# Splitting the rows of two gather layers into three bf16 parts, summed by three bf16 matmuls a column

## The chip, the core and the metric

The program runs on one core of one Trainium2 chip. Its engines are TensorE (PE; the profile lists its weight loads apart, as PEld), VectorE (DVE), ScalarE (ACT), GpSimd (POOL) and SyncE (SP), each with an instruction stream of its own; they meet only at semaphores. The metric is the device time of one execution, in microseconds (us); less is better.

## What is computed

A graph of 6250 nodes and 100000 edges, sorted by their end `dst`; a node has 256 features. After a layernorm and a relu come three SAGE layers, then a block of attention over the same edges. The three layers are what the change touches:

```python
def _sage_layer(x, src, dst, inv_deg, W_self, W_neigh, b):
    agg = jax.ops.segment_sum(x[src], dst, num_segments=N_NODES)
    mean = agg * inv_deg[:, None]
    return x @ W_self + mean @ W_neigh + b
deg = jax.ops.segment_sum(jnp.ones_like(src, dtype=features.dtype), dst, num_segments=N_NODES)
inv_deg = 1.0 / jnp.maximum(deg, 1.0)
h = relu(_sage_layer(features, src, dst, inv_deg, W0_self, W0_neigh, b0))
h = relu(_sage_layer(h, src, dst, inv_deg, W1_self, W1_neigh, b1))
h = _sage_layer(h, src, dst, inv_deg, W2_self, W2_neigh, b2)
```

## The kernel before

**Tiles, blocks and columns.** The nodes are NT = 49 tiles of 128. The edges are NB = 196 blocks of 512, and a block is BJ = 4 columns of 128 edges, one edge to a partition. Layer `l` (0, 1, 2; the title's two are 1 and 2) reads the rows `x[src]` out of a table in HBM, `tables[l]`, with one indirect DMA a column, issued by POOL (L763): 784 of them a layer. They land in `ring`, which has SLOTS = 7 slots of one block each.

**The sum over edges.** For a tile `t`, `sums(t)` on PE (L890 to L897) runs over the blocks that have edges of the tile. A block that lies over two tiles is walked twice, so a layer has 196 + 48 = 244 walks of 4 columns. For each column DVE makes a one-hot matrix (L842: edge by node of the tile), and PE multiplies it with the column's rows into `agg` (L895). One column of the rows' 257 words is the number 1, so the last column of `agg` is the node's degree. There are four one-hot buffers; DVE refills one when PE has used it (`onehot_used`).

**The rest of a tile.** DVE takes the mean (`means`, L948 to L953), PE transposes own rows and mean (`turn`, L904, L907), ACT copies them out (`take_turned`, L1016), PE multiplies with the weights (`products`, L913, L916), and ACT applies the relu into `h_nodes` (L1032). In the last layer the order is staggered over several tiles, and the projections of the attention (L1117 to L1168) run between.

**Who lets POOL go on.** SP relays: `landed` of a slot to PE (`rows_ready`, L790), and `onehot_used` to POOL (`slots_free`, L781), in one order: before it passes on block n it waits until block n + 4 - 7 has been used (AHEAD = 4).

**From one layer to the next.** The rows of a layer are the last layer's outputs, which ACT stores: eight tiles at a time, twice over, to `early_tables` (semaphore `stored`) and to `tables` (`last_stored`). The last tiles are stored one by one: tile 47 right behind its relu, tile 48 only to `tables`. The first LATE = 4 blocks of the next layer are gathered from `early_tables`, where tile 48's rows are zero, so POOL waits only for the stores of tiles 0 to 47; tile 48's rows are added into the ring afterwards, by one-hot matmuls on PE (`late_rows_tensor`, L717) and additions on DVE (`late_rows_vector`, L728). From the fifth block on POOL reads `tables` and waits for `last_stored`. The attention's gathers (L1278) start likewise from `vs_early`, stored by ACT at L1148. These are the lines of ACT's order at the end of layers 0 and 1, and POOL's first wait of a layer:

```python
                step(NT - 2)
                store(NT - 2)
                step(NT - 1)
                store(NT - 1)
...
                pool.wait_ge(W["stored"], since("stored", l, 0))
```

## Time and profile before

| | before |
|---|---|
| median of 3 runs (lowest to highest) | 4305.91 us (4305.18 to 4308.22) |
| the profiled execution, its own time | 4308.08 us |
| its span, first to last instruction | 4306.3 us |
| PE, DVE, ACT, POOL busy | 76%, 50%, 11%, 70% |
| mean granted TensorE clock | 0.89 of full |

The profiled execution's time is 1.8 us over its span, and 2.2 us over the median. POOL's busy time counts only the making of a DMA's descriptors; the 0.30 us between two gathers, in which it runs waits and register instructions, counts as idle "issue". In this execution layer 0's gathers end at 1018 us, layer 1's at 2000 us, layer 2's at 2982 us, and the attention's at 4018 us; what is behind is dense work. The page's chain covers only the last 20 us, so the place of the limit has to be read from the stages.

### The profile page before, as it was taken

Reading aid. Unit: us, or ns where it says so; the run is one execution under the profiler, and the core shown is the slowest. Engines: PE = TensorE matmul, PEld = TensorE weight load, DVE = VectorE, ACT = ScalarE, POOL = GpSimd, SP = SyncE. Lnnn points to the kernel's source line nnn. Section 1 sums busy time; section 2 is a strip of 40 time slices with the busy share of each in tenths; the row PEclk is TensorE's granted clock in tenths of the full one; section 3 lists DMA queues with packets and bytes.
Section 4 is the critical chain, followed back from the end, with each engine's and each line's share of the span. In section 5 each row is a group of like instructions: output and inputs, shape, how many; then the busy total and the mean of one; then the engine's idle time right before and its main releaser. Section 6 shows DMA issues by size and latency. Waiting matters only on the chain. (4 is left out here: it accounts for less than half of the span.)

```text
span 4306.3 us, 75198 instructions
## 1 busy us (share of the span) xinstructions
PE 3277.9 (76%) x13728; PEld 2372.7 (55%) x13729; DVE 2147.4 (50%) x6078; ACT 487.8 (11%) x1111; POOL 3020.7 (70%) x3154
## 2 busy tenths in 40 slices
PE   3777777777777777777788778887777777776798
PEld 2565555555555555555566555565655555555544
DVE  6434333333333333333455555545577777777733
ACT  4000000000000000000011101101011111111122
POOL 5777777777777777777777777776777777777200
PEclk9888889898888888888999999999888889898999
DMA  6444434435344344344444444445655555554411
GB/s 202 121 136 124 124 106 124 125 105 143 105 125 125 105 125 124 106 125 127 130 140 136 142 136 136 142 135 155 162 147 157 148 159 147 157 146 138 127 60 60
DMA packets 284796, 563.69 MB, mean 131 GB/s; under 512 B 104638, under 2 KB 176133, under 8 KB 279691
## 3 DMA queue, kind: packets, MB, share of 16 engines
q0 software_dynamic: 150528, 414.45, 34.0%
q10 hardware_dynamic: 70180, 89.46, 6.3%
q1 hardware_dynamic: 63974, 58.59, 4.4%
q8 instruction: 33, 0.54, 0.1%
q14 instruction: 81, 0.66, 0.0%
HBM read 487.19 MB, written 73.45 MB: 130 GB/s over the span
## 5 line engine op out<-in xcount | busy, mean ns | idle before, releaser
L763 POOL DMA_INDIRECT arena<-h_table,idx_v x2292 | 2174.3, 949 | 726.3 <-issue 694.0
L895 PE MATMUL banks<-arena 128*128 x5856 | 1544.9, 420 | 617.9 <-SPq L790 506.0
L895 PEld LDWEIGHTS banks<-arena 128*128 128x128 f32 x5856 | 1171.5, 208 | 957.2 <-issue 774.4
L842 DVE TENSOR_SCALAR arena<-iota_t,dst_e 128x128 f32<-128x128 f32 x2928 | 846.8, 310 | 821.7 <-PE banks L895 575.9
L1278 POOL DMA_INDIRECT arena<-vs_table,idx_v x764 | 765.0, 1001 | 232.8 <-issue 228.8
L1496 PE MATMUL banks<-arena 128*128 x1952 | 518.8, 416 | 52.8 <-DVE arena L1840 52.6
L1496 PEld LDWEIGHTS banks<-arena 128*128 128x128 f32 x1952 | 366.5, 199 | 192.5 <-issue 120.4
L916 PE MATMUL banks<-arena,lhs 128*128 128x256 f32 x1176 | 339.6, 439 | 5.0 <-ACT lhs L1016 0.2
L948 DVE TENSOR_SCALAR small<-banks 128x1 f32<-128x1 f32 x147 | 23.2, 158 | 638.7 <-PE banks L897 638.7
L1016 ACT ACTIVATE lhs<-banks 128x512 f32<-128x512 f32 x147 | 87.8, 597 | 2073.7 <-PE banks L907 2073.5
L916 PEld LDWEIGHTS banks<-arena,lhs 128*128 128x128 f32 x1176 | 240.5, 215 | 100.8 <-ACT lhs L1016 64.8
L1840 DVE SCALAR_TENSOR_TENSOR arena<-iota_n,tile_base,dst_e 128x256 f32<-128x256 f32 x488 | 224.0, 482 | 117.7 <-PE banks L1496 117.5
L1835 DVE TENSOR_TENSOR arena<-arena,banks (+1 forms) x196 | 238.9, 1219 | 31.0 <-issue 24.4
L907 PE MATMUL banks<-ident,tiles 128*128 128x128 f32 x294 | 69.4, 322 | 69.2 <-DVE tiles L953 69.2
L830 DVE TENSOR_SCALAR iota_t<-iota_n,tile_base 128x128 f32<-128x128 f32 x147 | 42.9, 292 | 153.5 <-issue 153.5
L913 PE MATMUL banks<-arena,ones_row 1*128 1x256 f32 x294 | 116.6, 480 | 0.0
L1125 PE MATMUL banks<-arena 128*128 128x512 f32 x196 | 92.3, 593 | 2.2 <-DVE arena L1158 2.2
L907 PEld LDWEIGHTS banks<-ident,tiles 128*128 128x128 f32 x294 | 36.0, 157 | 98.2 <-DVE tiles L953 98.2
L1968 PE MATMUL banks<-arena 128*128 (+2 forms) x208 | 86.2, 568 | 1.3 <-DVE arena L1923 1.3
L1978 PE MATMUL banks<-arena 128*128 128x512 f32 (+1 forms) x208 | 86.4, 568 | 0.2 <-DVE arena L1932 0.2
L1011 ACT ACTIVATE tiles<-arena 128x256 f32 (+1 forms) x147 | 61.2, 416 | 203.7 <-issue 195.6
L1621 ACT ACTIVATE arena<-banks 128x272 f32<-128x272 f32 x62 | 24.4, 394 | 510.5 <-PE banks L1498 510.5
(263 smaller groups left out, 2468.4 us busy)
## 6 DMA issues: line engine op xcount, KB each, us to landing
arena<-h_table,idx_v POOLq DMA_INDIRECT x2292
arena<-dst_dram SPq DMA_DIRECT2D x14, 1792.0 KB
arena<-vs_table,idx_v POOLq DMA_INDIRECT x764
h_table<-arena ACTq DMA_DIRECT2D x11, 1024.0 KB, 7.4
h_early<-arena ACTq DMA_DIRECT2D x10, 1024.0 KB
vs_table<-arena ACTq DMA_DIRECT2D x49, 132.0 KB
x_dram<-arena ACTq DMA_DIRECT2D x49, 128.0 KB
hln_dram<-arena ACTq DMA_DIRECT2D x49, 128.0 KB
```

Source lines behind the costliest of these rows:

```text
L763: pool.indirect_dma_start(ring[:, s * BJ + j, 0:width], None, table, bass.IndirectOffsetOnAxis(idx_v[:, half, n * BJ + j:n * BJ + j + 1], ...
L842: dve.tensor_scalar(onehot[:, j, :], iota_t[:], dst_e[:, bass.ds(b * BJ + j, 1)], None, ALU.is_equal).then_inc(W["onehot_made"], 1)
L895: pe.matmul(agg[:, 0:D + 1], onehot[:, j, :], ring[:, (b % SLOTS) * BJ + j, 0:D + 1], start=False, stop=False).then_inc(W["onehot_used"], 1)
L907: last = pe.transpose(tp[:, k, :], mean[:, k * P:(k + 1) * P], ident[:])
L913: pe.matmul(dense[:, 0:D], ones_row[:], b_sage[0:1, l, :], start=True, stop=False)
L916: last = pe.matmul(dense[:, 0:D], lhs[:, k, :], w_sage[:, l, k, :], start=False, stop=k == 2 * KD - 1)
L1016: act.activation(lhs[:], tp, ACT.Copy).then_inc(W["lhs_made"], 1)
L1125: pe.matmul(qk_ps, lhs_q[:, k, :], w_qkv[:, k, 0:2 * D], start=k == 0, stop=k == KD - 1)
L1278: pool.indirect_dma_start(v_ring[:, at, 0:VS], None, table, bass.IndirectOffsetOnAxis(idx_v[:, half, s * BJ + j:s * BJ + j + 1], 0)).then_ ...
L1496: pe.matmul(agg[:, 0:RW], onehot_v[:, j, :], v_ring[:, (b - (k - k % 2) * BB) * BJ + j, :], start=False, stop=False).then_inc(G["a_used"], 1)
L1835: dve.tensor_tensor(v, v, w.broadcast_to([P, BJ, HEADS, C]), ALU.mult).then_inc(G["rows_ready"], 1)
L1840: dve.scalar_tensor_tensor(onehot_v[:, j:j + 2, :], nodes_twice, tile_base[:, bass.ds(t, 1)], ends_of(b * BJ + j), ALU.add, ALU.is_equal). ...
```

## The change

In layers 1 and 2 a table row is no longer 256 fp32 words (1024 bytes) but three bf16 rows of 256, `hi`, `mid` and `lo` (1536 bytes), whose exact sum is the fp32 row. ACT writes `hi` with a second relu activation into a bf16 buffer `parts`, and DVE makes `mid` and `lo` (`split_vector`). A column's sum is three bf16 matmuls with one bf16 one-hot, which DVE makes from int16 node numbers. The additions of tile 48's rows go part by part: 12 rounds of 4 matmuls and 2 additions for 4. The degree's column falls away in layers 1 and 2: layer 0 keeps the inverse in `inv_deg`. `parts` holds two tiles, so ACT stores every tile by itself, twice, one tile behind: `store_parts(t - 1)` stands in `step(t)` behind `take_turned(t)`. Layer 0 sums as before but stores parts too. The diff's core:

```diff
--- before.py
+++ after.py
@@ -74,8 +74,10 @@
-    tables = [dram(f"h_table{i}", (NP, D)) for i in range(3)]
-    early_tables = [None] + [dram(f"h_early{i}", (NP, D)) for i in range(1, 3)]
+    PARTS = 3
+    PW = PARTS * D // 2
+    tables = [dram("h_table0", (NP, D))] + [dram(f"h_table{i}", (NP, PW)) for i in range(1, 3)]
+    early_tables = [None] + [dram(f"h_early{i}", (NP, PW)) for i in range(1, 3)]
...
+        ring = arena[:, o_ring:o_ring + ring_words].rearrange("p (s w) -> p s w", w=PW)
+        ring_parts = arena[:, o_ring:o_ring + ring_words].bitcast(BF16).rearrange("p (s m d) -> p s m d", m=PARTS, d=D)
...
+        hot16 = arena[:, o_free + 3 * D:o_free + 3 * D + BJ * P // 2].bitcast(BF16).rearrange("p (j n) -> p j n", j=BJ)
+        o_parts = o_free + 3 * D + BJ * P
+        parts_f = arena[:, o_parts:o_parts + 2 * PW].rearrange("p (i w) -> p i w", i=2)
+        parts = arena[:, o_parts:o_parts + 2 * PW].bitcast(BF16).rearrange("p (i m d) -> p i m d", i=2, m=PARTS)
...
+        left_over = hln
...
+        iota16 = iota_t[:, 0:P // 2].bitcast(I16)
...
+        inv_deg = rstd
...
-        LAST_STORES = 16 * (NT // GS + 2)
+        LAST_STORES = 16 * NT
...
         def late_rows_tensor(pe, l):
 
             pe.wait_ge(late_ends_made, LATE_STEPS + LATE)
-            pe.wait_ge(W["h_made"], since("h_made", l, 0))
-            for b in range(LATE):
-                if b > 1:
-                    pe.wait_ge(late_added, 2 * ((l - 1) * LATE + b - 1))
+            pe.wait_ge(parts_made, parts_at(l - 1, NT))
+            for r in range(LATE * PARTS):
+                b, m = r // PARTS, r % PARTS
+                if r > 1:
+                    pe.wait_ge(late_added, 2 * ((l - 1) * LATE * PARTS + r - 1))
                 for j in range(BJ):
-                    last = pe.matmul(banks[:, late_banks(l, b)[j // 2], (j % 2) * D:(j % 2 + 1) * D],
-                                     late_rows[:, b, j * P:(j + 1) * P], h_nodes[:, NT - 1, :], start=True, stop=True)
+                    last = pe.matmul(banks[:, late_banks(l, r)[j // 2], (j % 2) * D:(j % 2 + 1) * D],
+                                     late_rows[:, b, j * P:(j + 1) * P], parts[:, (NT - 1) % 2, m, :], start=True, stop=True)
                 last.then_inc(late_found, 1)
...
+        PARTS_FROM = NT + RAW * BJ
+        parts_made, part_step = ln_stats, ln_aggr
...
+        def split_vector(dve, l, t):
+
+            hi, mid, lo = (parts[:, bass.ds(t % 2, 1), m, :].rearrange("p o d -> p (o d)") for m in range(PARTS))
+            dve.wait_ge(W["h_made"], since("h_made", l, t + 1))
+            dve.tensor_tensor(left_over, h_nodes[:, t, :], hi, ALU.subtract).then_inc(part_step, 1)
+            dve.wait_ge(part_step, PARTS_FROM + 2 * (l * NT + t) + 1)
+            dve.tensor_copy(mid, left_over).then_inc(part_step, 1)
+            dve.wait_ge(part_step, PARTS_FROM + 2 * (l * NT + t) + 2)
+            dve.tensor_tensor(lo, left_over, mid, ALU.subtract).then_inc(parts_made, 1)
...
                     dve.wait_ge(W["onehot_used"], since("onehot_used", w, (b + t) * BJ + j + 1))
-                    dve.tensor_scalar(onehot[:, j, :], iota_t[:], dst_e[:, bass.ds(b * BJ + j, 1)], None,
+                    to, ids = (onehot, iota_t[:]) if w == 0 else (hot16, iota16)
+                    dve.tensor_scalar(to[:, j, :], ids, dst_e[:, bass.ds(b * BJ + j, 1)], None,
                                       ALU.is_equal).then_inc(W["onehot_made"], 1)
...
-            gathers(pool, l, D, may_fill)
+            gathers(pool, l, D if l == 0 else PW, may_fill)
...
-                        pe.matmul(agg[:, 0:D + 1], onehot[:, j, :], ring[:, (b % SLOTS) * BJ + j, 0:D + 1],
-                                  start=False, stop=False).then_inc(W["onehot_used"], 1)
...
+                        if l == 0:
+                            last = pe.matmul(agg[:, 0:width], onehot[:, j, :], ring[:, (b % SLOTS) * BJ + j, 0:width],
+                                             start=False, stop=False)
+                        else:
+                            for m in range(PARTS):
+                                last = pe.matmul(agg[:, 0:width], hot16[:, j, :], ring_parts[:, (b % SLOTS) * BJ + j, m, :],
+                                                 start=False, stop=False)
+                        last.then_inc(W["onehot_used"], 1)
...
             def means(t):
                 dve.wait_ge(W["agg_done"], since("agg_done", l, t + 1))
...
+                if l == 0:
+                    dve.tensor_scalar(small[:, 0:1], agg[:, D:D + 1], 1.0, None, ALU.max).then_inc(W["deg"], 1)
+                    dve.wait_ge(W["deg"], 2 * t + 1)
+                    dve.reciprocal(inv_deg[:, bass.ds(t, 1)], small[:, 0:1]).then_inc(W["deg"], 1)
...
             def step(t):
                 onehots(dve, l, t, *base_and_span(dve, l, t))
+                if there(t - 1):
+                    split_vector(dve, l, t - 1)
                 means(t)
...
-                if not isinstance(t, int) or t < NT - 1:
-                    act.dma_start(early[:, bass.ds(t, n), :], h_nodes[:, bass.ds(t, n), :]).then_inc(W["stored"], 16)
-                act.dma_start(to[:, bass.ds(t, n), :], h_nodes[:, bass.ds(t, n), :]).then_inc(last_stored[l], 16)
...
+            def store_parts(t):
+                act.wait_ge(parts_made, parts_at(l, t + 1))
                 if not isinstance(t, int) or t < NT - 1:
...
+                    act.dma_start(early[:, bass.ds(t, 1), :], parts_f[:, bass.ds(t % 2, 1), :]).then_inc(W["stored"], 16)
+                act.dma_start(to[:, bass.ds(t, 1), :], parts_f[:, bass.ds(t % 2, 1), :]).then_inc(last_stored[l], 16)
 
             def step(t):
                 own_rows(t)
                 take_turned(t)
+                if there(t - 2):
+                    act.wait_ge(W["stored"], since("stored", l, 16 * (t - 1)))
+                    act.wait_ge(last_stored[l], 16 * (t - 1))
+                if there(t - 1):
+                    store_parts(t - 1)
...
                 act.wait_ge(W["out_done"], since("out_done", l, t + 1))
                 apart(act)
+                act.activation(parts[:, bass.ds(t % 2, 1), 0, :].rearrange("p o d -> p (o d)"), dense[:, 0:D], ACT.Relu)
                 act.activation(h_nodes[:, t, :], dense[:, 0:D], ACT.Relu).then_inc(W["h_made"], 1)
...
-                with act.Fori(1, NT // GS - 1) as g:
-                    with act.Fori(g * GS, g * GS + GS) as t:
-                        step(t)
-                    store(g * GS, GS)
...
-                step(NT - 2)
-                store(NT - 2)
-                step(NT - 1)
-                store(NT - 1)
...
+                with act.Fori(GS, NT) as t:
                     step(t)
+                store_parts(NT - 1)
```

ACT at the end of layer 0, before: the stores of tiles 40 to 46 in one piece, then tiles 47 and 48 one by one. `lhs` is the copy of the transposed rows, the DMAs are the stores.

```order
L1024 DMA h_early<-arena 128x1792
L1025 DMA h_table<-arena 128x1792
L1011 ACTIVATE tiles<-arena 128x256
L1016 ACTIVATE lhs<-banks 128x512
L1032 ACTIVATE arena<-banks 128x256
L1024 DMA h_early<-arena 128x256
L1025 DMA h_table<-arena 128x256
L1011 ACTIVATE tiles<-arena 128x256
L1016 ACTIVATE lhs<-banks 128x512
L1032 ACTIVATE arena<-banks 128x256
L1025 DMA h_table<-arena 128x256
```

The same place now, with the semaphores waited for (`ln_stats` counts the finished splits): the loop of tiles 8 to 48, and the store of tile 48.

```order
L1063 ACTIVATE lhs<-banks 128x512 [waits out_done,turned]
L1079 ISA
L1070 REGISTER_ALU [waits last_stored0,stored]
L1072 ISA [waits ln_stats]
L1072 REGISTER_ALU
L1072 DMA h_early<-arena 128x384
L1073 DMA h_table<-arena 128x384
L1088 ISA [waits out_done]
L1088 ACTIVATE arena<-banks 128x256
L1089 ACTIVATE arena<-banks 128x256
...
L1073 DMA h_table<-arena 128x384 [waits ln_stats]
```

Tile 47's store to `h_early` stood behind tile 47's relu and ahead of all of tile 48's work; now it stands behind tile 48's copy to `lhs`.

PE in the loop over blocks, before, one column and the start of the next (ISA and REGISTER_ALU are register and wait instructions):

```order
L894 ISA [waits rows_ready]
L895 ISA [waits onehot_made]
L895 MATMUL banks<-arena 128x257
L894 REGISTER_ALU
L895 ISA [waits onehot_made]
L895 MATMUL banks<-arena 128x257
```

The same now, in layers 1 and 2:

```order
L928 REGISTER_ALU
L934 ISA [waits onehot_made]
L934 MATMUL banks<-arena 128x256
L934 ISA
L934 MATMUL banks<-arena 128x256
L934 ISA
L934 MATMUL banks<-arena 128x256
L928 REGISTER_ALU
```

A column was one fp32 matmul (two in the profile's count) with one ISA; it is three bf16 matmuls with three.

## Rows read from the trace of the kernel before

**Rows 1.** Stretches of layers 1 and 2: busy us (count), clock, DMA

```profile
core 0: us, PE busy (x) PEld busy (x) DVE busy (x) ACT busy (x) POOL busy (x), PEclk, DMA share, GB/s
1060.00:1998.00 938.00, 707.98 (x2667) 525.10 (x2666) 334.10 (x1143) 66.34 (x143) 709.79 (x750) 0.87 0.40 119
2040.00:2980.00 940.00, 758.03 (x3087) 557.56 (x3085) 476.33 (x1672) 96.59 (x231) 711.31 (x751) 0.96 0.47 137
```

**Rows 2.** The waits, longest in total first

```profile
POOL arena L763 <- issue: 703.7, 2309, 0.5
...
PE banks L895 <- SPq L790: 506.0, 200, 24.9
...
POOL arena L763 <- SPq L781: 32.4, 15, 27.2
```

**Rows 3.** POOL's timeline, from layer 0 to layer 1

```profile
1018.77 0.95 POOL L763 DMA_INDIRECT arena<-h_early,idx_v  x1 [0.30 <-issue]
...
1053.79 0.95 POOL L763 DMA_INDIRECT arena<-h_table,idx_v  x1 [0.30 <-SPq L781]
```

**Rows 4.** ACT's timeline, from layer 0 to layer 1

```profile
1012.82 0.35 ACTq L1024 DMA_DIRECT2D h_early<-arena  x1
...
1025.93 0.60 ACT L1016 ACTIVATE lhs<-banks 128x512 f32<-128x512 f32 x1 [11.77 <-PE banks L907]
```

**Rows 5.** From layer 1 to layer 2, the timelines of POOL, PE, DVE and ACT

```profile
2000.08 0.95 POOL L763 DMA_INDIRECT arena<-h_early,idx_v  x1 [0.30 <-issue]
...
2002.60 3.79 PE L895 MATMUL banks<-arena 128*128 x8 [3.31 <-SPq L790]
...
2006.65 0.16 DVE L948 TENSOR_SCALAR small<-banks 128x1 f32<-128x1 f32 x1 [6.82 <-PE banks L897]
...
2007.13 0.48 DVE L953 TENSOR_SCALAR tiles<-banks,small 128x256 f32<-128x256 f32 x1
...
2023.62 1.29 DVE L728 TENSOR_TENSOR arena<-arena,banks 128x512 f32<-128x512 f32 x2 [0.44 <-PE banks L717]
...
2008.39 0.60 ACT L1016 ACTIVATE lhs<-banks 128x512 f32<-128x512 f32 x1 [12.76 <-PE banks L907]
```

**Rows 6.** From layer 2 to the attention, the timelines of POOL, PE and ACT

```profile
2981.12 0.98 POOL L763 DMA_INDIRECT arena<-h_table,idx_v  x1 [0.30 <-issue]
2995.02 0.94 POOL L1278 DMA_INDIRECT arena<-vs_early,idx_v  x1 [12.91 <-DMA vs_early<-arena]
...
2985.62 2.00 PE L895 MATMUL banks<-arena 128*128 x8 [0.81 <-SPq L790]
...
2991.19 0.36 ACTq L1148 DMA_DIRECT2D vs_early<-arena  x1
```

**Rows 7.** POOL and DVE, timeline of layer 2, first and last of five longer gathers

```profile
2147.79 1.04 POOL L763 DMA_INDIRECT arena<-h_table,idx_v  x1 [0.30 <-issue]
...
2809.26 0.41 DVE L1160 TENSOR_TENSOR arena<-arena 128x256 f32<-128x256 f32 x1
2809.32 1.18 POOL L763 DMA_INDIRECT arena<-h_table,idx_v  x1 [0.30 <-issue]
```

**Rows 8.** Groups of instructions by form: count, busy us, mean ns

```profile
L1160 DVE TENSOR_TENSOR arena<-arena 128x256 f32<-128x256 f32 x49 | 20.3, 414 | 0.0
L1379 PE MATMUL banks<-arena 128*128 128x24 bf16 x784 | 27.5, 178 | 0.0
...
L1394 PE MATMUL banks<-zeros 128*128 128x480 bf16 x28 | 11.8, 421 | 1.5 <-DVE arena L1698 1.5
```

**Rows 9.** PE's timeline of layer 2: dense work of a tile, then the next tile

```profile
2606.50 0.38 PE L904 MATMUL banks<-ident,tiles 128*128 128x128 f32 x2
...
2612.28 0.27 PE L890 MATMUL banks<-zeros 128*128 128x257 bf16 x1
```

**Rows 10.** The gathers by line: duration in ns, least/median/most

```profile
L763 POOL DMA_INDIRECT arena<-h_table,idx_v x2292: 942/946/1804, 68.7 to 2981.1; - x191
...
L1278 POOL DMA_INDIRECT arena<-vs_table,idx_v x764: 942/946/4447, 3020.7 to 4017.2; - x191
```

More of the change, by code:

```diff
@@ L721, in late_rows_vector @@
         def late_rows_vector(dve, l):
-            for b in range(LATE):
-                dve.wait_ge(landed[b], since("landed", l, 16 * BJ))
-                dve.wait_ge(late_found, l * LATE + b + 1)
+            for r in range(LATE * PARTS):
+                b, m = r // PARTS, r % PARTS
+                if m == 0:
+                    dve.wait_ge(landed[b], since("landed", l, 16 * BJ))
+                dve.wait_ge(late_found, LATE + (l - 1) * LATE * PARTS + r + 1)
                 for i in range(2):
-                    rows = ring[:, b * BJ + 2 * i:b * BJ + 2 * i + 2, 0:D]
-                    dve.tensor_tensor(rows, rows, banks[:, late_banks(l, b)[i], :].rearrange("p (j d) -> p j d", d=D),
+                    rows = ring_parts[:, b * BJ + 2 * i:b * BJ + 2 * i + 2, m, :]
+                    dve.tensor_tensor(rows, rows, banks[:, late_banks(l, r)[i], :].rearrange("p (j d) -> p j d", d=D),
@@ L733, in gnn_kernel @@
                      onehot_made=BJ * PAIRS, base_moved=NT, agg_done=NT, deg=2 * NT, mean_made=NT, self_made=NT,
-                     turned=NT, lhs_made=NT, out_done=NT, h_made=NT, stored=16 * (NT // GS + 1), landed=16 * BJ * ROUNDS)
+                     turned=NT, lhs_made=NT, out_done=NT, h_made=NT, stored=16 * (NT - 1), landed=16 * BJ * ROUNDS)
         W = {n: sem(n) for n in TOTAL if n != "landed"}
@@ L829, in base_and_span @@
                 dve.wait_ge(W["onehot_made"], since("onehot_made", w, (b0 + t) * BJ))
-            dve.tensor_scalar(iota_t[:], iota_n[:], tile_base[:, bass.ds(t, 1)], None, ALU.add).then_inc(W["base_moved"], 1)
+            dve.tensor_scalar(iota_t[:] if w == 0 else iota16, iota_n[:], tile_base[:, bass.ds(t, 1)], None, ALU.add).then_inc(W["base_moved"], 1)
             return b0, b1
@@ L889, in sums @@
                 wait(pe, W["mean_made"], since("mean_made", l, t))
-                pe.matmul(agg[:, 0:D + 1], zeros[:, 0:P], zeros[:, 0:D + 1], start=True, stop=False)
+                width = D + 1 if l == 0 else D
+                pe.matmul(agg[:, 0:width], zeros[:, 0:P], zeros[:, 0:width], start=True, stop=False)
                 with pe.Fori(b0, b1 + 1) as b:
@@ L970, in step @@
                 onehots(dve, l, t, *base_and_span(dve, l, t))
+                if there(t - 1):
+                    split_vector(dve, l, t - 1)
                 means(t)
             def last_layer_step(t):
+                if isinstance(t, int) and t == 3:
+                    dve.wait_ge(last_stored[1], LAST_STORES)
                 def between():
@@ L997, in sage_vector @@
                     step(t)
+                split_vector(dve, l, NT - 1)
             else:
@@ L1001, in sage_vector @@
                     first_and_rest(dve, NT, step)
+                    split_vector(dve, l, NT - 1)
                 else:
@@ L1029, in step @@
                 take_turned(t)
+                if there(t - 2):
[3 more added lines that the diff above has]
+                    store_parts(t - 1)
+                if l == 1 and isinstance(t, int) and t == 0:
+                    act.wait_ge(W["stored"], since("stored", l, 0))
+                    act.wait_ge(last_stored[0], LAST_STORES)
                 act.wait_ge(W["out_done"], since("out_done", l, t + 1))
                 apart(act)
+                act.activation(parts[:, bass.ds(t % 2, 1), 0, :].rearrange("p o d -> p (o d)"), dense[:, 0:D], ACT.Relu)
                 act.activation(h_nodes[:, t, :], dense[:, 0:D], ACT.Relu).then_inc(W["h_made"], 1)
```

44 lines of the change are left out of this document (21 added, 23 removed).

## The prediction

> **What bounds the kernel now.** I read the stretches first. In layers 1 and 2 POOL makes 750 gathers in 938 us and 751 in 940 us, one each 1.25 us, whatever the other engines do in between (PE 708 us, then 758 us) [rows 1]. One gather is 946 ns of work and 0.30 us of issue. Then the waits: POOL's idle time ahead of the gathers is almost all its own issue (703.7 us), and its waits for a free slot come to 32.4 us in 15 times; PE waits 506.0 us for gathered blocks [rows 2]. So the limit is POOL, which runs without a stop from layer to layer: the first gather of layer 1 starts at 1018.77, and that of layer 2 at 2000.08, each after the usual 0.30 us of issue [rows 3, 5]. The one real stop, 12.91 us ahead of the attention, waits for the store `vs_early` [rows 6]. A faster matmul buys nothing here unless it shortens a stop of POOL; a new stop costs its whole length.
>
> **The store that moves (layer 0 to 1).** Before, tile 47 was stored to `h_early` at 1012.82, ahead of tile 48's work, and POOL went on at 1018.77 [rows 3, 4]. Now `store_parts(47)` stands behind tile 48's `lhs` copy, which runs from 1025.93 for 0.60 us [rows 4]. That copy needs tile 48's whole sum, hence the layer's last gather landed, and POOL waits for the store ahead of its next gather. The copy ends at 1026.53; the two waits of stores two tiles back and the wait for the split have long been met. From issue of such a store to POOL's gather there are 2995.02 - 2991.19 = 3.83 us in the one place that shows it, with 1056 bytes a partition instead of 1536 [rows 6]. POOL resumes at 1030.4 instead of 1018.77: **+11.6 us**. Layer 0 still sums in fp32, so nothing shortens this. Bounds: 9.5, if a store behind nothing else lands sooner, and 14, if the wider store lands 2 us later.
>
> **The same, layer 1 to 2.** PE starts the last block's four columns when they land, at 2002.60; its 8 records of fp32 take 3.79 us, at the low one of the two clock levels, and the same work takes 2.00 us at the high one [rows 5, 6]. Twelve bf16 matmuls replace them. No row has one of 256 columns: 24 columns take 178 ns, 480 take 421 ns, so 0.53 ns a column of the moving side, 0.14 us a matmul [rows 8], 1.6 us for twelve; but each now comes with a register instruction of its own, so I take 2.4 (bounds 1.6, and 12 times half of a low-level fp32 record with its share of issue, 12 x 0.24 = 2.9). The sum ends 1.4 us sooner. The degree's two operations fall away, 2007.13 - 2006.65 = 0.48 us [rows 5]. The 1.5 times larger gather lands later, estimated 0.2 us. The `lhs` copy, from 2008.39 to 2008.99 before, ends at 2007.3; plus 3.83 gives 2011.1 against 2000.08: **+11.1 us** (9 to 13).
>
> **What hides the rest of the passage.** Tile 48's rows now take 12 rounds: 24 additions, 6 a block, at 1.29 / 2 = 0.65 us [rows 5]. Counted from POOL's restart: the fourth block is issued at +20, lands 2985.62 - 2982.10 = 3.5 us later [rows 6], its six additions end at +27.4, the first column can be summed at +28, and the first block is used at about +31. POOL needs that slot for the eighth block at +35. So about 4 us of slack, and no term; before, POOL waited for this slot just visibly, at 1053.79 [rows 3]. Behind PE's late rounds only its own sums are queued; behind DVE's additions the one-hots, counted above.
>
> **Layer 2 to the attention.** The last block's matmuls took 2.00 us there, at the high level [rows 6], against my 2.4; +0.2 for landing, -0.48 for the degree. Sum **0** (-1 to +1.5).
>
> **Splits beside the gathers.** Each of 98 tiles adds two `tensor_tensor` with both inputs in SBUF and a cast, some 0.4 us each. They sit between the tile's one-hots and its mean; PE and DVE have the time, since PE waits for gathers. What counts is POOL. The comparable operation is L1160, 49 times 414 ns [rows 8]. Where one was running as a gather started, the gather took 1.18 us instead of 0.94: the operation ended 0.35 us into the gather, 0.24 were lost [rows 7]. Five gathers of layer 2 that started under an L1160 took between 1.01 and 1.18 us, together 0.83 us over the usual, so 17 ns an operation: 196 of them would give 3.3 us. But L1160 has a fixed place in time behind a landing; one at a random place would be hit with 0.43 / 1.25 = 0.34, losing 0.15 or so, 10 us in all; and a place just ahead of each gather would cost 0.25 x 98 = 25. I take **+8** (0 to +25), nearer to random, since the split follows one-hots that PE's progress sets. The shorter int16 one-hots may give back 1.
>
> The Trainium skill, "SBUF — State Buffer", section "Who interferes with whom", speaks against this change: a VectorE instruction with two SBUF inputs contends with a GpSimd one that reads SBUF, and the second to issue blocks until the first is done. By that rule alone, at random places, the sum would have 196 x 0.34 x 0.215 = 14 us, an estimate, instead of 8. The row of 1.18 us agrees in kind: the gather behind the operation waited, though not for the operation's whole rest.
>
> **Sum.** 11.6 + 11.1 + 0 + 8 - 1 = 29.7 us. The profiled execution, 4308.08 us (4306.3 of span and 1.8 around it), becomes 4337.8; it is 2.2 above the median of the runs, so the median becomes 4335.6, say **4336 us**, 0.7% slower. Gathers themselves are counted at no change: going from 1024 to 1056 bytes a row left the median at 946 ns [rows 10], and the descriptors' number is that of the rows.
>
> **Rivals.**
> - *PE becomes the bound.* In layer 2 a tile's dense work holds PE from 2606.50 to 2612.28, 5.8 us at the high level [rows 9]. POOL delivers a tile's four blocks in 20.0 us, and PE walks 244 / 49 = 4.98 blocks, so it may take (20.0 - 5.8) / 4.98 = 2.85 us a block, 0.71 a column. Before, a column took 2.00 / 4 = 0.50 at most. Three matmuls with three register instructions: below, 3 x 0.14 = 0.42; above, three times what one fp32 record now takes with all its issue, 3 x 0.25 = 0.75. At 0.75 layer 2 grows by 0.04 x 976 = 39 us and the whole to 4375. For it: PE's granted clock may be lower with less to do, and layer 2 has most dense work. Against: a column would have to spend most of its time on issue, and a PE that falls behind is busy, and has the high level, as in layer 2 (0.96) [rows 1]. 0.12.
> - *Wide rows slow the gathers.* If 1536 bytes cost POOL 0.05 us each, 1568 of them give 78 us: 4414. Against: [rows 10], and DMA engines busy 0.40 to 0.47 [rows 1], which at 1.5 times the gathers' bytes stay under 0.7. 0.05.
> - *The other side: POOL doesn't stop.* If the wait for tile 47's store were met in time, 11.6 and 11.1 fall away, and with splits that miss the gathers (0 for 8) the time is 4306 - 1 = 4305: not slower. To be faster by over 0.2% it would have to give back more than the sum holds. It decides where the store is issued 4 us ahead of POOL's need; ACT's order puts it 8 us behind (1026.56 against 1018.77) [rows 3, 4]. 0.05.
> - *The split's place is the worst one*, ahead of each gather: 25 instead of 8, 4353. 0.08.
>
> **How the numbers follow.** My forecast holds 0.70, the rivals 0.12, 0.05, 0.05 and 0.08. The range reaches from 4322 (both passages and the splits at their lower bounds: 9.5 + 9 - 1 + 0 - 1 = 16.5) to 4368, over the worst place of the split and most of what PE could add. A measurement tells 0.2%, 8.6 us, from no change. Slower by that: 0.94; within: 0.04; faster: 0.02.
>
> **What would show it.** POOL should stop once at each passage, 10 to 12 us, released by the store to `h_early`, and otherwise keep 1.25 us a gather, with a few hundredths of a microsecond more on average where a split runs. PE's share should fall in layer 1, with its waits for blocks grown. The wait ahead of the attention should stay near 13 us. Waits of POOL for a slot in layer 2 would mean the first rival; a median over 950 ns the second; no stop the third; gathers of 1.1 to 1.3 us once or twice in every tile the fourth.

## The result, and the profile after

The change makes the kernel 0.74% slower: median 4338.02 us of 4 executions (4335.15 to 4340.43) against 4305.73 (4305.18 to 4308.22, 4 executions), ratio 1.0074, 95% interval 1.0056 to 1.0091. The profiled execution took 4340.43 us, with a span of 4338.6, which is 32.3 more than before; the granted TensorE clock was 0.88. All of this is from the condition in which the kernel before takes some 4310 us; ten of the twelve runs below met another, in which it takes 6560, and the two must not be mixed.

POOL's timeline at the three passages. First the last gathers of layers 0 and 1 in the kernel before, which were not shown:

```profile
1017.52 0.95 POOL L763 DMA_INDIRECT arena<-h_table,idx_v  x1 [0.30 <-issue]
...
1998.83 0.95 POOL L763 DMA_INDIRECT arena<-h_table,idx_v  x1 [0.30 <-issue]
```

The same of the changed kernel, with the gather behind each:

```profile
1020.41 0.95 POOL L795 DMA_INDIRECT arena<-h_table,idx_v  x1 [0.30 <-issue]
1032.24 0.95 POOL L795 DMA_INDIRECT arena<-h_early,idx_v  x1 [10.89 <-issue]
...
2019.62 0.95 POOL L795 DMA_INDIRECT arena<-h_table,idx_v  x1 [0.30 <-issue]
2031.13 0.95 POOL L795 DMA_INDIRECT arena<-h_early,idx_v  x1 [10.56 <-issue]
...
3011.47 0.94 POOL L795 DMA_INDIRECT arena<-h_table,idx_v  x1 [0.30 <-issue]
3027.48 0.94 POOL L1329 DMA_INDIRECT arena<-vs_early,idx_v  x1 [15.07 <-DMA vs_early<-arena]
```

From start to start a passage took 1.25 us before and takes 11.83 and 11.51 now: +10.6 and +10.3. The one ahead of the attention took 13.90 [rows 6] and takes 16.01: +2.1. The rest lies in the stretches between. From its first gather to its last, layer 1 took 1998.83 - 1018.77 = 980.1 us and takes 2019.62 - 1032.24 = 987.4, so +7.3; layer 2 went from 981.0 to 980.3. Behind the last passage nothing changed (1311.3 us, then 1311.1). What remains of the 32.3 us, 2.9, is layer 0.

Windows of the changed kernel, behind the passages, answer to [rows 1] (busy us and count of each engine, clock, DMA):

```profile
1073.00:2019.00 946.00, 724.65 (x3620) 445.99 (x3619) 351.98 (x1191) 74.87 (x192) 717.43 (x751) 0.85 0.62 176
2072.00:3011.00 939.00, 792.71 (x4037) 475.23 (x4035) 445.89 (x1578) 96.60 (x231) 710.43 (x751) 0.95 0.67 189
```

Layer 2 keeps 1.25 us a gather with rows half as wide again, 189 GB/s and a DMA share of 0.67. Layer 1 has 1.26, with the same rows. So the width costs POOL nothing (experiments 3 and 4 show it in layer 1 too); what the two layers differ in is the split, which only layers 0 and 1 have. The waits of the changed kernel answer to [rows 2]:

```profile
POOL arena L795 <- issue: 726.0, 2314, 10.9
...
PE banks L930 <- SPq L822: 206.9, 83, 24.0
PE banks L934 <- DVE arena L875: 194.1, 254, 2.2
...
PE banks L934 <- SPq L822: 163.7, 80, 3.1
```

POOL's two stops are in the "issue" row, as its longest; the profile found no releaser for them, so experiments 1 and 2 have to show what they wait for.

**The store, from layer 0 to 1 and from 1 to 2** (timelines of PE and ACT; before: [rows 4, 5], and the first line here, PE at the last block of layer 0):

```profile
1021.27 2.86 PE L895 MATMUL banks<-arena 128*128 x8 [3.33 <-SPq L790]
...
1019.00 8.25 PE L930 MATMUL banks<-arena 128*128 x32
...
1029.03 0.60 ACT L1063 ACTIVATE lhs<-banks 128x512 f32<-128x512 f32 x1 [8.83 <-PE banks L947]
1029.51 0.34 ACTq L1072 DMA_DIRECT2D h_early<-arena  x1
...
2023.87 2.48 PE L934 MATMUL banks<-arena 128*128 x12 [2.08 <-SPq L822]
...
2027.95 0.60 ACT L1063 ACTIVATE lhs<-banks 128x512 f32<-128x512 f32 x1 [12.11 <-PE banks L947]
2028.44 0.35 ACTq L1072 DMA_DIRECT2D h_early<-arena  x1
```

The `lhs` copy starts 8.6 us behind the start of the layer's last gather at the first passage and 8.3 at the second; 0.5 us later the store is issued, and 2.73 and 2.69 us after that POOL's gather starts.

**A gather under a split** (timelines of DVE and POOL, layer 1):

```profile
1192.97 0.42 DVE L757 TENSOR_TENSOR arena<-arena 128x256 f32 x1 [0.23 <-issue]
1193.02 1.19 POOL L795 DMA_INDIRECT arena<-h_table,idx_v  x1 [0.30 <-issue]
...
1315.44 0.50 DVE L761 TENSOR_TENSOR arena<-arena 128x256 f32 x1
1315.49 0.94 POOL L795 DMA_INDIRECT arena<-h_table,idx_v  x1 [0.30 <-issue]
```

The trace's records have the nanoseconds. In the first pair the subtraction started 57 ns ahead of the gather, and the gather took 1187 ns. In the second it started 43 ns ahead; here the subtraction took the loss (499 ns in place of 425) and the gather its usual 942. By the same records 32 gathers of layer 0 and 48 of layer 1 started under one of the three operations of a split. Of these, 17 and 34 took over 975 ns (I call them long), in all 3.2 and 6.9 us more than 946 ns each.

**PE in front of the attention** (PE's timeline, then ACT's store; before: [rows 6]):

```profile
3012.65 2.03 PE L934 MATMUL banks<-arena 128*128 x12 [1.69 <-DVE arena L875]
3015.27 2.05 PE L934 MATMUL banks<-arena 128*128 x12 [0.59 <-DVE arena L875]
3017.91 2.02 PE L934 MATMUL banks<-arena 128*128 x12 [0.59 <-DVE arena L875]
...
3023.90 0.37 ACTq L1199 DMA_DIRECT2D vs_early<-arena  x1
```

Twelve matmuls take 2.04 us and the next twelve start 0.59 later: 2.64 us a walk of a block, 0.66 a column, where fp32 took 2.0 us a walk.

### The profile page after: what moved, and what is told of

Read it like the earlier page. It is cut to its first block and busy times, and to the rows that moved or that the text cites. A ratio compares the mean times of both kernels' runs of the same rounds, so it can differ in the third digit from the quotient of the medians.

```text
span 4338.6 us, 84744 instructions
## 1 busy us (share of the span) xinstructions
PE 3333.8 (77%) x15710; PEld 2192.6 (51%) x15713; DVE 2209.7 (51%) x6208; ACT 505.0 (12%) x1209; POOL 3029.1 (70%) x3154
## 5 line engine op out<-in xcount | busy, mean ns | idle before, releaser
L795 POOL DMA_INDIRECT arena<-h_table,idx_v x2292 | 2183.6, 953 | 726.3 <-issue 695.8
L875 DVE TENSOR_SCALAR arena<-iota_t,dst_e 128x128 bf16<-128x128 int16 (+1 forms) x2928 | 805.0, 292 | 954.7 <-PE banks L934 539.0
L934 PEld LDWEIGHTS banks<-arena 128*128 128x128 bf16 x5856 | 592.8, 101 | 800.2 <-issue 500.6
L930 PE MATMUL banks<-arena 128*128 x1952 | 528.8, 428 | 227.2 <-SPq L822 206.9
L930 PEld LDWEIGHTS banks<-arena 128*128 128x128 f32 x1952 | 396.9, 211 | 349.4 <-issue 288.5
L1547 PEld LDWEIGHTS banks<-arena 128*128 128x128 f32 x1952 | 368.5, 200 | 194.4 <-issue 121.5
L956 PE MATMUL banks<-arena,lhs 128*128 128x256 f32 x1176 | 349.8, 449 | 5.1 <-ACT lhs L1063 0.8
L994 DVE TENSOR_SCALAR tiles<-banks,rstd 128x256 f32<-128x256 f32 x147 | 71.1, 484 | 318.7 <-PE banks L947 159.6
L862 DVE TENSOR_SCALAR iota_t<-iota_n,tile_base 128x128 int16<-128x128 f32 (+1 forms) x147 | 45.0, 306 | 138.7 <-issue 138.7
```

The source lines that it names most:

```text
L795: pool.indirect_dma_start(ring[:, s * BJ + j, 0:width], None, table, bass.IndirectOffsetOnAxis(idx_v[:, half, n * BJ + j:n * BJ + j + 1], ...
L875: dve.tensor_scalar(to[:, j, :], ids, dst_e[:, bass.ds(b * BJ + j, 1)], None, ALU.is_equal).then_inc(W["onehot_made"], 1)
L930: last = pe.matmul(agg[:, 0:width], onehot[:, j, :], ring[:, (b % SLOTS) * BJ + j, 0:width], start=False, stop=False)
L934: last = pe.matmul(agg[:, 0:width], hot16[:, j, :], ring_parts[:, (b % SLOTS) * BJ + j, m, :], start=False, stop=False)
L956: last = pe.matmul(dense[:, 0:D], lhs[:, k, :], w_sage[:, l, k, :], start=False, stop=k == 2 * KD - 1)
L1547: pe.matmul(agg[:, 0:RW], onehot_v[:, j, :], v_ring[:, (b - (k - k % 2) * BB) * BJ + j, :], start=False, stop=False).then_inc(G["a_used"], 1)
```

## The experiments

The two conditions, by the kernel before in the same session on the chip: **A**, 4306 to 4315 us, clock 0.89; **B**, 6558 to 6690 us, clock 0.72. It isn't the chip alone: one chip showed A in one session and B in another.

| kernel | condition | median us | before us | ratio (95%) |
|---|---|---|---|---|
| changed | A | 4338.0 | 4305.7 | 1.0074 (1.0056 to 1.0091) |
| store first | A | 4326.8 | 4308.4 | 1.0043 (1.0029 to 1.0056) |
| store first, split in PSUM | A | 4319.8 | 4315.4 | 1.0013 (1.0003 to 1.0022) |
| changed | B | 6365.2 | 6558.0 | 0.971 (0.969 to 0.974) |
| store first | B | 6360.3 | 6559.0 | 0.969 (0.967 to 0.971) |
| split in PSUM | B | 6385.0 | 6559.0 | 0.974 (0.972 to 0.976) |
| narrow rows | B | 6352.1 | 6559.0 | 0.968 (0.964 to 0.971) |
| two matmuls | B | 6566.9 | 6565.2 | 1.001 (0.999 to 1.003) |
| before, stores behind (3 runs) | B | 6579 to 6586 | 6558 to 6571 | 1.003 each |
| before, values early | B | 6741.0 | 6689.6 | 1.007 (1.005 to 1.010) |
| all three edits | B | 6401.8 | 6565.2 | 0.976 (0.974 to 0.978) |

**1. The store first** (DVE's last step, with the split behind the first block of one-hots, and ACT's, with the store ahead of the tile's work):

```diff
...
+            def last_step():
+                t = NT - 1
+                onehots(dve, l, t, *base_and_span(dve, l, t), behind_first=lambda: split_vector(dve, l, t - 1))
...
+            def last_step():
+                t = NT - 1
...
+                store_parts(t - 1)
+                own_rows(t)
+                take_turned(t)
...
```

> The changed kernel, with the store of tile 47's parts moved ahead of all of tile 48's ACT work in each gather layer, and the split of tile 47 moved behind the first block of one-hots of tile 48. My theory: the two stops of POOL ahead of layers 1 and 2 (10.89 and 10.56 us) come from the place of this store alone. Then POOL starts the first gather of layer 1 and of layer 2 after the usual 0.3 us of issue, and the time falls by 10.6 + 10.3 = 20.9 us, to 4317 us. Rival: the longer work of the last tile (the split, the wider store, the last block's bf16 sums) holds POOL as well; then a stop of 3 us or more stays at each passage and the time falls by less than 15 us, to over 4323 us.

The first run met condition B; its stops are read in experiment 6. The second:

> The changed kernel with the early store of tile 47 alone, as in its first run, which met a chip on which PE was the bound. Where POOL is the bound (kernel before at some 4310 us): the run with both edits had no stop at either passage, but a wait of 2.3 us for a ring slot some 35 us into layer 1. If the place of the store makes the stops, this kernel has the same two passages, its layer 1 keeps the slower pace of the changed kernel (947 us for the last 751 gathers against 941), and the time is 19 to 21 us below the changed kernel and some 5 us above the run with both edits. If the stops depended on the split's operands, stops of 3 us or more return. Where PE is the bound (kernel before at some 6560 us), it repeats 0.97.

It met A: 4326.8 us. The timelines of PE, ACT and POOL at the first passage:

```profile
1009.36 2.83 PE L930 MATMUL banks<-arena 128*128 x8 [2.98 <-SPq L822]
...
1019.26 0.38 ACT L1095 ACTIVATE arena<-banks 128x256 f32 x1 [4.47 <-PE banks L956]
...
1021.28 0.37 ACTq L1079 DMA_DIRECT2D h_early<-arena  x1
...
1021.50 0.95 POOL L795 DMA_INDIRECT arena<-h_table,idx_v  x1 [0.30 <-issue]
1025.29 0.94 POOL L795 DMA_INDIRECT arena<-h_early,idx_v  x1 [2.84 <-issue]
```

The stop fell from 10.89 to 2.84 us here and from 10.56 to 3.19 at the second passage, by 15.4 us in all, not by 20.9: I had named 3 us or more as the rival's, and the time is over the rival's 4323. It is 11.2 us under the changed kernel, where I had expected 19 to 21. So the place of the store makes the larger part of the stops, but moving it leaves no slack. Tile 47's store needs that tile's relu, and here PE did that tile's work partly at the low clock level (2.83 us for a block that takes 2.00 at the high one). The relu ended 3.1 us ahead of POOL's need, and from there to POOL's gather it takes 1025.29 - 1019.64 = 5.65 us.

**2. Store first, and the split's remainder in PSUM.** With experiment 1 this changes where `left_over` lies, and what the first operation reads:

```diff
...
-        left_over = hln
+        left_over = banks[:, 3, 0:D]
...
-            dve.tensor_tensor(left_over, h_nodes[:, t, :], hi, ALU.subtract).then_inc(part_step, 1)
+            dve.scalar_tensor_tensor(left_over, dense[:, 0:D], 0.0, hi, ALU.max, ALU.subtract).then_inc(part_step, 1)
```

> The changed kernel with both edits: the store of tile 47 and its split ahead of the last tile's work, and the split with its remainder in PSUM. On a chip whose TensorE clock lets POOL be the bound, as in the two profiles on record (kernel before 4306 us): the two stops (20.9 us) and the slower pace (10 us) both go, and the time is 4307 us, level with the kernel before; if splits with SBUF inputs don't cost POOL anything, it is 4317. On a chip that grants less clock, as the first four experiments met (clock 0.72 against 0.89, kernel before 6559 us), PE is the bound and the time is 0.97 of the kernel before, as in the two experiments that hold one edit each.

Condition A, 4319.8 us: 4.4 over the kernel before, interval 0.03% to 0.22%. The timelines of PE, ACT and POOL at the passage and behind it, and of DVE and POOL where a split's first operation runs as a gather starts:

```profile
1006.81 2.00 PE L930 MATMUL banks<-arena 128*128 x8 [1.16 <-SPq L822]
...
1013.35 0.38 ACT L1095 ACTIVATE arena<-banks 128x256 f32 x1 [2.30 <-DMA h_early<-arena]
...
1018.75 0.95 POOL L795 DMA_INDIRECT arena<-h_table,idx_v  x1 [0.30 <-issue]
1020.00 0.95 POOL L795 DMA_INDIRECT arena<-h_early,idx_v  x1 [0.30 <-issue]
...
1057.35 0.95 POOL L795 DMA_INDIRECT arena<-h_table,idx_v  x1 [2.59 <-SPq L813]
...
1222.77 0.43 DVE L757 SCALAR_TENSOR_TENSOR banks<-banks,arena 128x256 f32<-128x256 f32 x1 [0.21 <-issue]
1222.85 0.94 POOL L795 DMA_INDIRECT arena<-h_table,idx_v  x1 [0.31 <-issue]
```

The windows of layer 0 and layer 1 of the same kernel:

```profile
112.00:1018.50 906.50, 679.74 (x2561) 499.98 (x2560) 391.67 (x1274) 71.31 (x183) 686.99 (x720) 0.87 0.44 128
1060.00:1999.00 939.00, 716.90 (x3619) 437.79 (x3619) 353.57 (x1188) 73.91 (x189) 710.67 (x750) 0.87 0.61 177
```

I had expected it level with the kernel before. The passage is back to 0.30 us: the relu ended 1020.00 - 1013.73 = 6.3 us ahead of POOL's need, more than the 5.65 us that it takes; experiment 1 had (1021.50 + 1.25) - 1019.64 = 3.1. The split's other operands aren't what did it: from the relu's end to the store's issue there are 1.6 us in experiment 1 and 1.8 here. What differs is PE, which did tile 47's block in 2.00 us. The second passage is back to 0.31. Layer 1 is back to 1.25 us a gather although there are as many split operations, and as long ones, as in the changed kernel: one with a PSUM operand started 79 ns ahead of a gather, and the gather took 945 ns. In all, 32 gathers of layer 0 and 79 of layer 1 started under a split operation here, and none took over 954 ns. This settles the second cause for both layers: it is the split operations that work in SBUF alone, not DVE's being busy. Layer 0 as a whole came back by half only: from first to last gather it took 948.9 us before, 951.9 in the changed kernel and 950.4 here, still 1.26 us a gather. That rest isn't in gathers under a split. The usual gather of this execution takes 949 ns, in layers with and without a split, where the kernel before has 946, and 756 times 3 ns are 2.3 us. The stop that is gone gave 2.3 us back: POOL now waits for a ring slot at 1057.35, since the late rows have less time. The other cost that remains is the one ahead of the attention, 3002.75 - 2986.78 = 15.97 us from start to start, as long as in the changed kernel.

**3. The split in PSUM alone**

> The changed kernel, with what is left over of a split kept in PSUM and the first of the three operations reading the tile's result from PSUM, so that no operation of the split has both inputs in SBUF. The number of operations, the stores and the width of the gathers stay. My theory: the gathers of layers 0 and 1 are slower by 2.9 and 7.3 us in all because split operations with SBUF inputs run as gathers start; they then return to 1.25 us each and the time falls by about 10 us, to 4328 us. Rival: the wider stores and rows (1536 bytes) slow layers 0 and 1; then the time stays at 4338 us. Second rival: VectorE's writes count whatever their inputs; it stays at 4338 us too, and the narrow-row kernel tells the two apart.

Condition B. POOL waits for slots there, so the time can't tell; experiment 2 answers in its place. But the trace tells how long the gathers themselves take. The views of the line L795 in layer 1, with the least, median and longest gather in ns, of the changed kernel (experiment 8), of this one and of the narrow rows (experiment 4), all in B:

```profile
L795 POOL DMA_INDIRECT arena<-h_table,idx_v x768: 943/949/1202, 1625.8 to 2965.6; - x192
...
L795 POOL DMA_INDIRECT arena<-h_table,idx_v x768: 942/949/972, 1609.7 to 2955.7; - x192
...
L795 POOL DMA_INDIRECT arena<-h_table,idx_v x768: 940/946/1201, 1622.7 to 2968.3; - x192
```

Of layer 1's 784 gathers 47 are long in the changed kernel, 9.3 us over 946 ns together, and 46 of these started under a split operation. With this edit alone none is, although 89 started under one. With narrow rows and the split in SBUF 39 are, 7.4 us. So the operands make the long gathers, and not the width of the rows. With the store first and the operands in SBUF 46 are long in B, so it isn't the place of the store either.

**4. Narrow rows** (gathers 1024 bytes; sums part 1 twice in place of `lo`)

```diff
...
-            gathers(pool, l, D if l == 0 else PW, may_fill)
+            gathers(pool, l, D, may_fill)
...
-                                last = pe.matmul(agg[:, 0:width], hot16[:, j, :], ring_parts[:, (b % SLOTS) * BJ + j, m, :],
+                                last = pe.matmul(agg[:, 0:width], hot16[:, j, :], ring_parts[:, (b % SLOTS) * BJ + j, min(m, 1), :],
```

> The changed kernel, gathering 1024 bytes of a row in layers 1 and 2 in place of 1536 (it leaves out the third part lo, and sums part mid twice to keep three matmuls a column; the late rows keep their twelve rounds). It has the split, its place and the stores of the change. My theory, that the width of a row costs POOL nothing: the time stays within 3 us of 4338. Rival, that the width accounts for the slower pace of layer 1 (7.3 us): the time falls by about 7 us or more, to 4331 or less, and layer 1 returns to 1.25 us a gather.

Condition B, 6352 us, 0.1 to 0.5% under its companions on the same chip. The gathers' median is 946 ns here and 949 in the changed kernel in B, but that is no matter of width: each of the two has the same median in layer 0, where both gather 1024 bytes, and the wide rows of experiment 7 have 946. What the time does in A wasn't measured; layer 2 of the changed kernel, above, is the answer there.

**5. Two matmuls a column** (leaves the part `lo` out of the sums)

```diff
...
-                            for m in range(PARTS):
+                            for m in range(PARTS - 1):
```

> The changed kernel with two of the three matmuls a column (the sums leave out the third part lo; gathers, split and late rows stay). Where POOL is the bound: my theory is that matmuls matter only at the passages; the stop ahead of layer 2 shrinks by about 0.6 us (a block's walk from 2.64 to some 2.0 us), the one ahead of the attention from 15.1 to about 13, where PE is one block behind the landings, and all else stays: 4335 us. Rival: PE's walk of 0.66 us a column, close to the 0.71 that I worked out as the point where it binds, delays slots of the ring and explains the slower pace of layer 1 (947 us for 751 gathers); then layer 1 returns to 941 and the time falls by 6 us more, to 4329. Where PE is the bound (kernel before at some 6560 us): a quarter to a third less matmul work in two layers, and a time clearly under 0.97 of the kernel before.

Condition B: 1.001, and my expectation there, clearly under 0.97, was wrong. With a third of the sums' matmuls taken away the kernel is slower than with all of them (0.971, on another chip; in the same session on the same chip the kernel with all three edits and three matmuls took 6401.8 us against 6566.9), at a lower clock (0.696 against 0.725). So I don't understand condition B as a plain lack of PE's time. Whether the third matmul is what lengthened the stop ahead of the attention wasn't tried in A; the rows above show only that three walks of 2.64 us stand there one behind another.

**6. The kernel before with the stores behind** (fp32 throughout; only the order of the stores is the changed kernel's)

```diff
...
                 take_turned(t)
+                if there(t - 1):
+                    store(t - 1)
...
```

The stores of eight tiles at a time, and those of tiles 47 and 48 behind their own steps, go in turn; only tile 48's stays at the end.

> The kernel before (fp32 rows, fp32 sums, no split) with the changed kernel's order of stores: each tile stored by itself, one tile behind, after the copy of the next tile's lhs. My theory: the place of the store alone makes the two stops; POOL stops for 10 to 12 us at each of the two passages, and the time rises by 20 to 23 us, to 4326 to 4329 us. Rival, that the stops belong to the split or the three wide parts: the time stays at 4306 us, or rises by less than 10.

> The kernel before (fp32 rows and sums, no split) with the changed kernel's order of stores, as in the first run of it, which met a chip on which PE was the bound. Where POOL is the bound (kernel before at some 4310 us): if the place of the store alone makes the two stops, POOL stops 10 to 12 us ahead of layer 1 and of layer 2, and the time rises by 20 to 23 us. If the stops belong to the split or the wider parts, the time rises by less than 10 us.

> The kernel before with the changed kernel's order of stores, a third time, since both earlier runs met chips on which POOL waits for ring slots (kernel before 6559 and 6571 us). Where POOL is the bound (kernel before at some 4310 us): if the place of the store alone makes the two stops, POOL stops 10 to 12 us ahead of layer 1 and of layer 2 and the time rises by 20 to 23 us; if they belong to the split or the wider parts, by less than 10. On a chip of the other kind: 1.003 again.

All three met B: 1.0028, 1.0030, 1.0031. The cost of that order without a split was never measured in A. The stops themselves can be read in B. POOL's timelines, from layer 0 to 1: the kernel before's own order (experiment 7's second kernel, whose layers 0 and 1 are unchanged), this one (third run), the changed kernel, and experiment 1's:

```profile
1622.36 0.95 POOL L763 DMA_INDIRECT arena<-h_early,idx_v  x1 [10.04 <-issue]
...
1577.64 0.94 POOL L763 DMA_INDIRECT arena<-h_early,idx_v  x1 [17.70 <-issue]
...
1605.50 0.95 POOL L795 DMA_INDIRECT arena<-h_early,idx_v  x1 [20.78 <-issue]
...
1595.89 0.95 POOL L795 DMA_INDIRECT arena<-h_early,idx_v  x1 [13.31 <-issue]
```

From layer 1 to 2 the stops are 10.13, 18.39, 24.57 and 13.71 us. So in B POOL stops at a passage even in the old order; the new order alone, with fp32 and no split, has stops longer by 7.7 and 8.3 us, and putting the store first in the changed kernel takes 7.5 and 10.9 off. The first of the four is from a session in which the kernel before took 6690 us, the others are from ones with 6558 or 6559, so the first difference is only as good as that.

**7. Values early, in layer 2** (DVE and ACT do tile t - 4's projection ahead of tile t's mean)

```diff
...
+                    if there(t - 4):
+                        project_vector(dve, t - 4)
                     means(t)
...
```

> The run with both edits (early store of tile 47, remainder of the split in PSUM) and a third one: the projection of tile t-4 and the store of its values stand ahead of the means and transposes of tiles t and t-1 in layer 2. My theory: the stop ahead of the attention (15.0 us in the changed kernel, for the store to vs_early) lasts as long as the last such store stands behind the last tiles' sums; moved ahead of them it shrinks to 5 us or less, a later wait for vs_table takes 2 to 4 us, and the time is 7 to 8 us below the run with both edits, hence 0.998 to 1.000 of the kernel before. Rival: the attention waits for the last tile's own values soon after anyway; then the wait only moves and the ratio stays at 1.001 or more. Where PE is the bound (kernel before at some 6560 us): 0.97, as the single edits gave.

> The kernel before, with the projection of tile t-4 and the store of its values in layer 2 ahead of the means and transposes of tiles t and t-1, as in the earlier run that had this beside the two other edits. Where POOL is the bound (kernel before at some 4310 us): my theory is that the stop ahead of the attention (12.9 us, for the store to vs_early) shrinks to 5 us or less, a later wait takes 2 to 4 us, and the ratio is 0.998. Rival: the wait only moves on to the values of the last tile; the ratio is 1.000. On a chip of the other kind (6560 us) neither is told apart, and the ratio is 1.00.

Both met B. With the two other edits the ratio is 0.976, not better than without; alone on the kernel before, 1.007, against my 1.00. The stop ahead of the attention is still 27.3 and 27.8 us there against 25 to 32 in the other kernels of B, so the edit didn't remove it, and nothing speaks for it.

**8. The changed kernel in condition B**

> The changed kernel itself, on the chip of this call. Where POOL is the bound, it repeats 1.0074 of the kernel before, within its interval (1.0056 to 1.0091). On a chip of the other kind, where the variants of it with one edit each gave 0.969 and 0.974, it gives 0.97: faster, not slower.

0.971, as expected: the change that costs 0.7% in A saves 2.9% in B. No kernel tried beats the kernel before in A; in B the changed kernel with the store first is as good as any (0.969).

## Why the prediction was right

The forecast was 4336 us, the range 4322 to 4368, and the time 4338.0. The cause and its three main terms were right; that the time came so close is in part luck. In the profiled execution the sum was 29.7 us and the growth 32.3: the two passages came out 1.8 us short, the splits and the wait ahead of the attention 2.2 and 2.1 us long. Step by step:

- **The store, 0 to 1**: +11.6 forecast, 10.6 measured. The chain was the one named, but for its start: PE didn't wait for the last block to land. It ran the tile's last four blocks without a pause (the 32 records above), late because it had done tile 47 at the low clock level. That its sum ended about as far behind the last gather as before is chance. I had the copy end at 1026.53 in the old time; in the new it started 8.6 us behind the last gather's start, as before (1025.93 - 1017.52 = 8.4). What I over-sized was the time from issue to POOL: 3.83 from the one row I had, but 2.73 here, and ACT issued the store 0.1 us ahead of the copy's end. That the place of the store is the cause is shown by experiment 1 (-8.0 and -7.4) and by experiment 2, in which both stops are gone.
- **1 to 2**: +11.1, measured 10.3. The walk was estimated at 2.4 us and took 2.48; again 2.69 in place of 3.83. Against that, the last block landed 0.5 us later, not 0.2: PE took it up 2023.87 - 2019.62 = 4.25 us behind the last gather's start, where it had been 2002.60 - 1998.83 = 3.77.
- **No stop later in the layers**: right in the changed kernel, but the slack of 4 us was less than that: without the stop, 2.3 us of it were missing (experiment 2), at the place that I had named, the slot for the eighth block.
- **Layer 2 to the attention**: 0 (-1 to +1.5) forecast, +2.1 measured, outside its bounds. The step that failed is that I took only the last block's matmuls. PE stands behind by the two blocks before it as well: fp32 did the first two in 3.7 us without a gap, three bf16 walks take 2.64 each, and the first waited for its one-hots. The last walk starts 6.4 us behind the last gather's start, not 4.5 [rows 6].
- **Splits beside the gathers**: +8 forecast, 2.9 + 7.3 measured. The gathers that started under a split operation took 3.2 + 6.9 us more than 946 ns each, and with the operands in PSUM nothing of that is left (experiment 2), so the cause holds in both layers. Their number is as I had it: 65 gathers started under the 196 subtractions, a share of 0.33 against my 0.34, and lost 0.15 us each; the casts lost another 0.5 us.
- **Their place**: near random, I had said, and it isn't. In layer 1 of the changed kernel a gather under a split took what was left of the operation at its start plus 0.82 us: 368 left gave 1187, 281 gave 1102, 189 (a cast) gave 1007. With 946 ns as the usual time this is as if a gather ran some 0.13 us before it is held, and an operation that ends in that time costs nothing. Of a subtraction and a gather within some 45 ns either may lose. By this a subtraction at a random place would lose (0.38 - 0.13)² / 2 / 1.25 = 0.025 us, 2.7 us a layer with the casts, an estimate. Layer 0 with 3.2 is near it. Layer 1 lost 6.9, for 27 gathers started under its 49 first subtractions, and 20 of these within 46 to 144 ns of the subtraction's start. So my 0.15 us a hit was too much for random places and came true because the places weren't random. The Trainium skill ("SBUF — State Buffer", "Who interferes with whom") has the second to issue blocked until the first is done. The trace agrees in kind, though a gather doesn't lose the first 0.13 us. With the page's rule, 14 us, the time would have been 4342, an estimate: within the range as well.
- **The shorter one-hots**: -1 forecast. One-hots lengthen gathers too: in the kernel before 18 long gathers of layer 1 and 13 of layer 2 had started under one, 0.8 and 0.6 us in all. In the changed kernel it is 4 and 1, 0.2 us together, so some 1.2 us came back.
- **Rivals**: PE didn't become the bound in A, but it came near: 0.66 us a column against the threshold of 0.71 in layer 2, nearer my upper bound (0.75) than the lower (0.42). Wide rows cost nothing. POOL did stop. The split's place in layer 1 was between random (2.7 us a layer) and the worst (25 us for all 98 tiles).
- **The signs**: two were wrong. PE's share in layer 1 should have fallen, but it rose from 707.98 / 938.00 = 0.75 to 724.65 / 946.00 = 0.77, and its waits for blocks should have grown, but they fell from 506.0 us to 206.9 + 163.7. A walk takes 2.64 us where fp32 takes 2.00 at the high level, and even the 2.4 that I had taken for it is more than that. Nor does the profile name the store as what released POOL.

## What to carry to other kernels

Where one engine issues without a pause, look for what it waits for at each passage, and at where that store now stands in its engine's order: a store moved behind the next tile's copy cost more here than all the added operations. A DVE operation that works in SBUF alone, as the split's subtractions and cast do, costs POOL time only where a gather starts under it; here one operand in PSUM took that away. Before a change is judged, run the kernel before in the same session: by the condition met, this change is 0.7% slower or 2.9% faster.

## What the runs showed that I had not expected

In condition B the engines don't take turns as the waits say. The kernel before with its stores behind (third run), layer 1, timelines of POOL, PE and DVE:

```profile
2133.01 0.94 POOL L763 DMA_INDIRECT arena<-h_table,idx_v  x1 [0.30 <-issue]
2146.09 0.95 POOL L763 DMA_INDIRECT arena<-h_table,idx_v  x1 [12.14 <-SPq L781]
...
2125.18 0.42 PE L897 MATMUL banks<-zeros 128*128 128x257 bf16 x1
...
2123.55 0.45 DVE L842 TENSOR_SCALAR arena<-iota_t,dst_e 128x128 f32<-128x128 f32 x1 [1.84 <-PE banks L895]
2136.83 0.16 DVE L948 TENSOR_SCALAR small<-banks 128x1 f32<-128x1 f32 x1 [12.83 <-remote]
```

PE's sum ended at 2125.6, all that L948 waits for by the code, yet DVE ran it 11.2 us later, 2.9 us after POOL's last gather of a run of 16 had ended; in A the same step follows within 0.1 us. Until then POOL had filled the ring, and afterwards it waits 12 us for slots. This repeats: in this trace DVE's L948 has 123 waits of this kind ("remote" in the view), 1483 us in all, and POOL 245 waits for slots, 1697 us. In the changed kernel it shows as single matmuls with 0.3 to 2.5 us of "issue" between them until POOL stops. It looks as if something that POOL's gathers use held back the other engines' instructions in B; this is read from when things happen, and no run tests it. The low clock doesn't explain it: PE is idle in these holes, and in the first 100 us of the first of the three runs, at a granted clock of 0.97, PE's busy time was already half of that of the kernel before in A (17.8 against 36.4 us, the latter at 1.00). Whether it is the fetching of instructions, and what sets the condition from session to session, no run here tells; it is left open.
